# Attention softmax: where the row maximum is subtracted and the row sum taken

## The reference

```
q = (xn @ Wq) -> 16 heads of 64, scaled          k, v = xn @ Wkv   (one k and v of 64 for all heads)
k, v get one extra null column (null_kv, from cond_64)
sim  = q k^T + bias[h]                           (null column: null_attn_bias[h])
sim  = -max where the causal mask or the key mask hides the column
attn = softmax(sim);  out = layernorm((attn @ v) @ Wo)
```

## Time and profile before

| | us |
|---|---|
| median of 3 runs | 925.21 |
| lowest and highest run | 918.31, 926.66 |
| the profiled execution's own time | 919.85 |
| its span, first to last instruction | 918.1 |

### The profile page before, as it was taken

The page is one execution under the profiler, slowest core; times in us unless marked ns, Lnnn a source line. Parts: engine busy times, 40 slices in busy tenths (PEclk is TensorE's granted clock), DMA queues, the critical chain, the costliest instruction groups (busy, mean ns, idle before and its releaser), DMA issues. The chain is left out here.

```text
span 918.1 us, 14493 instructions
## 1 busy us (share of the span) xinstructions
PE 692.0 (75%) x4394; PEld 628.4 (68%) x4395; DVE 484.8 (53%) x1127; ACT 287.8 (31%) x643; POOL 356.0 (39%) x466
## 2 busy tenths in 40 slices
PE   1466677620579999659899999945489889999990
PEld 1356667510478989527788888724489889999990
DVE  3354545458611111156877777748267557766640
ACT  1214424410023233124233333233235424544320
POOL 2122021000034445412344443223385567676672
PEclk9666675565679999969999999976799999999995
DMA  8372092030039998249401000020363352222234
GB/s 260 78 161 46 21 296 106 0 112 4 0 103 312 304 298 247 36 143 353 155 19 35 17 17 0 14 79 0 118 140 95 61 137 37 43 43 46 44 45 112
DMA packets 78386, 94.98 MB, mean 103 GB/s; under 512 B 8480, under 2 KB 69344, under 8 KB 78176
## 3 DMA queue, kind: packets, MB, share of 16 engines
q1 hardware_dynamic: 64160, 76.80, 27.0%
q0 software_dynamic: 11536, 14.94, 9.8%
q10 hardware_dynamic: 2640, 2.62, 0.9%
HBM read 77.68 MB, written 18.56 MB: 105 GB/s over the span
## 5 line engine op out<-in xcount | busy, mean ns | idle before, releaser
L1320 PE MATMUL f_pt<-xparts,cparts 128*128 128x512 f32 x480 | 119.2, 398 | 0.0
L1857 ACT ACTIVATE nh<-npH,c_sb 128x288 f32<-128x288 f32 x128 | 64.1, 501 | 121.0 <-PE npH L1829 121.0
L1320 PEld LDWEIGHTS f_pt<-xparts,cparts 128*128 128x128 f32 x480 | 88.7, 191 | 18.5
L1775 POOL DMA_INDIRECT acc<-nyg,si x51 | 91.3, 1790 | 13.9 <-issue 13.6
L108 POOL TENSOR_TENSOR held<-ones 128x1 f32<-128x1 f32 x134 | 48.5, 362 | 109.4 <-DVE nyg L1876 53.2
L1308 POOL TENSOR_TENSOR hidl<-sums,hidh 128x512 fp32r<-128x512 f32 x40 | 52.1, 1302 | 93.3 <-ACT hidh L1362 93.3
L1827 PE MATMUL npH<-nxh,w1l 128*128 128x288 f32 x256 | 77.9, 304 | 1.6 <-DVE nxl L1869 1.6
L1838 PE MATMUL npY<-nhh,w2l 128*128 128x288 f32 x256 | 78.3, 306 | 0.0
L1840 PE MATMUL npY<-nhh,w2h 128*128 128x288 f32 x256 | 76.7, 300 | 0.0
L1839 PE MATMUL npY<-nhl,w2h 128*128 128x288 f32 x256 | 76.6, 299 | 0.0
L1829 PE MATMUL npH<-nxh,w1h 128*128 128x288 f32 x256 | 76.3, 298 | 0.0
(11 more groups left out here) (345 smaller groups left out, 1510.7 us busy)
## 6 DMA issues: line engine op xcount, KB each, us to landing
w_sb<-in_w SPq DMA_DIRECT2D x32, 1024.0 KB, 8.4
w_sb<-in_v SPq DMA_DIRECT2D x16, 1024.0 KB, 10.5
bias_sb<-in_bias SPq DMA_DIRECT2D x4, 1024.0 KB, 12.8
acc<-zrow SPq DMA_DIRECT2D x1, 2056.0 KB, 16.4
sums<-acc SPq DMA_DIRECT2D x4, 514.0 KB, 5.3
x_sb<-in_x SPq DMA_DIRECT2D x1, 2048.0 KB, 9.9
table<-row ACTq DMA_DIRECT2D x1, 2048.0 KB, 14.6
b_sb<-in_b SPq DMA_DIRECT2D x1, 2048.0 KB, 8.2
```

The lines of the kernel that those rows point to most:

```text
L1320: ins = pe.matmul(pp[:, c % 2], cparts[:, u, wn, at], xparts[:, xn, k, chunk], start=(k == 0 and (wn, xn) == (0, 1)), stop=(k == KD - 1 an ...
L1775: pool.indirect_dma_start(acc1, bass.IndirectOffsetOnAxis(ap=si3[:, s:s + 1], axis=0), yg[:, s], None, compute_op=ALU.add).then_inc(scatte ...
```

## The change

DVE subtracts the running maximum from the group's 512 scores in place (`shifted`), and tells ACT by a new semaphore. ACT takes one exponential of 512 columns per group, without bias and without accumulation, and increments `p_ready` by 4 at once. DVE takes the row sums of the four groups (`summed`) after it has scaled O and LEN. `shifts` still computes both DIF and NEG.

```diff
-            KSTEP = 20
-            NEGATED = (5, 9, 13, 16)
+            KSTEP = 24
+            sub_ready = sem("t_sub_ready")
...
                         def exps(g):
-                            act.wait_ge(k_step, done(nk * KSTEP + NEGATED[g]))
-                            for h in heads(g):
-                                act.activation(sc[:, h], sc[:, h], ACT.Exp, bias=st[:, NEG, h:h + 1],
-                                               accum_out=st[:, RS, h:h + 1]).then_inc(p_ready, 1)
+                            act.wait_ge(sub_ready, nk * 4 + g + 1)
+                            act.activation(by_bank(sc[:], g), by_bank(sc[:], g), ACT.Exp).then_inc(p_ready, 4)
...
+                        def shifted(g):
+                            dve.tensor_tensor(by_bank(sc[:], g), by_bank(sc[:], g), bcast(mine[g][TMAX], P),
+                                              ALU.subtract).then_inc(sub_ready, 1)
+
+                        def summed(g, step):
+                            dve.wait_ge(p_ready, nk * 16 + 4 * g + 4)
+                            put(step, dve.tensor_reduce(mine[g][RS], by_bank(sc[:], g), AX, ALU.add))
...
                         shifts(0, 4, 2)
+                        shifted(0)
                         add(2)
                         joined(1, 6, 3)
                         largest(2, 7)
                         shifts(1, 8, 6)
+                        shifted(1)
                         add(3)
                         joined(2, 10, 7)
                         largest(3, 11)
                         shifts(2, 12, 10)
+                        shifted(2)
                         joined(3, 14, 11)
                         shifts(3, 15, 14)
+                        shifted(3)
...
                         put(19, dve.tensor_tensor(st[:, LEN], st[:, LEN], st[:, ALPHA], ALU.mult))
-                        dve.wait_ge(k_step, done(at + 19))
-                        put(20, dve.tensor_tensor(st[:, LEN], st[:, LEN], st[:, RS], ALU.add))
+                        for g in range(4):
+                            summed(g, 20 + g)
+                        dve.wait_ge(k_step, done(at + 23))
+                        put(24, dve.tensor_tensor(st[:, LEN], st[:, LEN], st[:, RS], ALU.add))
```

## The result

The change makes the kernel slower. Twenty runs of each gave a median of 930.2 us (925.63 to 937.82) against 924.0 (914.25 to 939.32); the ratio is 1.0093, 95% interval 1.0071 to 1.0115. That ratio leaves out the runs of each kernel that lie over 1.5% above its own fastest, which are six of the kernel before and none of the changed one; the two medians of all twenty runs stand at 1.0067. Timed again later beside three other kernels the ratio was 1.0055 (1.0022 to 1.0088). Together that is +5 to +9 us, where the forecast's sum was +1.4.

What follows compares the result with a forecast made beforehand. ACT bounded the middle of a tile, TensorE its end. Tiles 1 and 2 at +3.2 us and tiles 3 and 4 at -1.84 made +1.4: 926.6 on the median, 923.9 on the average; forecast 925, range 917 to 931.

Steps and rivals of the forecast that it cites:

- the exponentials' starts: In tile 1, ACT's four wide exponentials were to start at 70.85, 72.9, 74.95 and 75.95 us.
- a weighing: In tile 1, TensorE's weighing matmuls of one group were given 0.9 us, the first ending at 77.55.
- 0.94 us earlier: TensorE was to end its last weighings of tile 1 at 80.35 us, where 81.29 was before.
- tiles 3 and 4: Tile 4 was to begin 0.94 us earlier and end 0.9 us earlier, together -1.84 us.
- The hand-over of the path to DVE: At a tile's end, DVE instead of TensorE was to finish last, 0.60 us later than before.
- Costs of DVE's and ACT's instructions: Per tile: DVE's eight added operations 0.60 us each, group cycle 2.06; ACT's wide exponential 0.62.
- POOL's additions holding up DVE's final scaling: In tiles 1 and 2, POOL's earlier bias additions were to delay DVE's final scaling of O by about 1.0 us each.
- Rival B, the clock: TensorE no longer gets its high clock in each query tile: +6.7 us with the sum, 932; chance 0.13.
- A: Shared ports do not matter, DVE goes first or POOL starts later: sum -0.64 us, 924.6 on the median; chance 0.20.
- C: ACT's saving of 3.7 us a tile arrives whole, 15 us in four tiles: 910; chance 0.03.
- The 1% bound: For the whole kernel, 9.3 us was about what a measurement can tell from no change; no change got 0.92.

Runs made afterwards that it cites:

- e1: The changed kernel with each 512-column exponential counting its semaphore up by 1 instead of 4, waits scaled to match; ratio to the kernel before 1.0055.
- e8: e1 with the first three of the four row sums moved ahead of DVE's wait for ALPHA; ratio to the kernel before 1.0013.
- e4: The kernel before with 12 idle transposes of the identity on TensorE between the scores and first transposes of each key tile; ratio 1.0020.
- r1b: The kernel before, nothing changed, profiled a second time; attention stage 137.2 us.
- r5: The changed kernel, unaltered, timed again beside three other kernels; ratio to the kernel before 1.0055, attention stage 137.1 us.
- r7: The kernel before, nothing changed, profiled a fifth time; attention stage 131.3 us.
- e2: The kernel before with each one-head exponential counting its semaphore up by 2 instead of 1, TensorE's wait doubled; ratio 1.0054.
- e3: The kernel before with only the row sums moved to DVE behind ALPHA, exponentials one head at a time with bias, without accumulation; ratio 1.0032.
- e7: The changed kernel with exponentials one head at a time, accumulating and without bias, and no sums on DVE; ratio to the kernel before 1.0059.

## Why the prediction was wrong, step by step

Two terms of the sum failed, and both made TensorE's part too early: the exponentials' starts left out the table load, and a weighing was given 0.9 us where it takes 1.6 to 1.8. With them fell the "0.94 us earlier" of TensorE, on which the -1.84 us of tiles 3 and 4 rested. TensorE's last weighings came 0.50 us later, not 0.94 earlier.

**The exponentials' starts: failed.** "Exponentials: 70.85, 72.9, ..." left out the table load. The forecast looked at what each wait holds back on its engine, but not at where the load goes once the instruction behind the wait is another. It is 0.41 us a tile (e1 against the changed kernel), 1.6 in all.

**The weighings: mis-sized.** "Weighing 1 to 77.55" gives a group 0.9 us. The 1.99 of the earlier trace rows for 16 is the high level, while the 1.05 that it gave the transposes is the low one: two levels were mixed in one unbroken run. The timeline of TensorE in the kernel before, tile 1, has 8 such matmuls at 1.81, and the next transposes start 1.60 after them:

```profile
73.48 1.11 PE L498 MATMUL pT<-ident,sc 128*128 128x128 f32 x4 [0.80 <-ACT sc L553]
74.39 1.81 PE L504 MATMUL pO<-vblk,PT 128*128 128x64 f32 x8
75.99 1.06 PE L498 MATMUL pT<-ident,sc 128*128 128x128 f32 x4
76.84 1.81 PE L504 MATMUL pO<-vblk,PT 128*128 128x64 f32 x8
```

With 1.6 to 1.8 TensorE has no gap from its second transposes on even in the kernel before, and from there it, not ACT, was the bound. So the "0.94 us earlier" of TensorE did not come: in e1, where the load is out of the way, its first weighing starts at +7.16 of the tile, before at +7.06, since the second group's exponential has to wait for DVE. ACT's saved 3.7 us bought nothing there. That also delays ALPHA (+10.35 in e1, forecast +9.92), and with it DVE's tail: at the high level e1 has 15.68, the forecast 15.29 and the changed kernel 16.09. The 0.39 of this step and the 0.41 of the load are the whole of the difference for a tile at the high level.

**The hand-over of the path to DVE: half right.** It holds at the high level only (tail 0.83 by e8); at the low level TensorE still ends the tile. The costs a tile are then +0.50 low (16.71 against 16.21) and +1.33 high (16.09 against 14.76). The forecast had +0.60, for the high level.

**Costs of DVE's and ACT's instructions: right.** Sums 2.46 for four, cycle 2.06, subtractions 0.68 to 0.69, the wide exponential 0.63 for a forecast 0.62.

**POOL's additions holding up DVE's final scaling: right in kind, wrong in place and size.** In tile 1 they came 2.0 us later from the tile's start, not 0.94 earlier, so in the first profile the scaling was ahead as before. In e1, where tile 1 was high and TensorE ended before DVE, it happened. Timelines of DVE and POOL:

```profile
82.65 1.57 DVE L738 TENSOR_TENSOR O<-O,st 128x1024 f32<-128x1024 f32 x1
```
```profile
81.87 5.92 POOL L431 TENSOR_TENSOR bias_sb<-bias_sb,comb 128x512 f32 x4
```

The scaling took 1.57 instead of 1.22, held by the rest of POOL's first addition: 0.35 us, in the changed kernel 0.28 and 0.26 in two of its five profiles (1.50 and 1.48), not 1.0 in each of two tiles. A loss of the forecast's size came once, in tile 1 of e4, where POOL's additions start at 81.65 (timeline of DVE, e4):

```profile
81.64 2.35 DVE L729 TENSOR_TENSOR O<-O,st 128x1024 f32<-128x1024 f32 x1
```

The rule that the forecast named from the Trainium skill ("SBUF — State Buffer", on the two separate sides) agrees with these rows; it was the starting times that were wrong.

**Tiles 3 and 4: wrong sign.** Tile 4 should have begun 0.94 us earlier. TensorE's last weighing decides that, and it came later. From the start of tile 3 to the start of tile 4 it is 19.57 us for 19.07 (low, the changed kernel's first profile against r1b) and 17.82 for 17.30 (high, r5 against r7).

**Rival B, the clock: it happened, by more than its share.** It had 0.13. Its price was right (3.51 for 1.99, 3.57 for 1.94), but it was taken for a property of the program. It varies in both kernels, and the prediction rested on one execution's rows as if they were typical: three of four tiles high.

**Rivals A and C** did not come. A's condition, DVE first, was met in the first profile, but its sum rested on the same early TensorE.

By sizes: the change costs 2.0 us where all four tiles run low (4 x 0.50) and about 3.6 where the first three run high. That is 1.33 in each of tiles 1 and 2, and 0.94 from the start of tile 3 to the end of tile 4 (35.23 us in r5, 34.29 in r7): DVE's longer tail in tile 3 is mostly hidden, since tile 4 begins when the scores are there. What was measured beyond that goes with TensorE's level in the tiles and between them, and whether the change itself shifts that level stays open. The 1% bound held (0.93% and 0.55%, though the first interval reaches 1.15%), the direction was slower, and that the range of 917 to 931 held the median of 930.2 was luck: it was wide for the spread between executions, not for these two steps.

## What to carry to other kernels

When the instruction that first uses an ACT table changes its wait or its semaphore count, look in the trace whether the table load runs ahead of the wait or behind it: 1.28 us that were free ahead of a wait can land behind it. An engine's saved time is worth what the next engine leaves idle; add up the next engine's unbroken run first, at the clock level of its own rows. And profile the kernel before more than once when a few microseconds are in question: one execution's clock levels made 7.6 us here.

## What the hardware showed that was not expected

- A semaphore count above 1 on the exponential that follows the table load came with the wait on the load, in the changed kernel and in e2; with a count of 1 it stood on the exponential (the kernel before, e1, e3, e7, e8).
- Exponentials of 128 columns start 0.386 us apart with a bias column and an accumulated sum, 0.30 with the bias alone (e3), 0.29 with the sum alone (e7). Both together cost 0.09 more than either alone; no run has exponentials of this width with neither.
- The same TensorE instructions at the same place of a tile took 1.99 or 3.52 us in different executions of one program, at granted clocks of 1.00 and 0.50.
